# Local attention: probabilities in three transposed banks, edge rows of V by transfers, and the output product ahead of the values' projection

## The reference

```python
qkv = shift_token(x) @ wqkv
q, k = rotary_xpos(l2norm(q) * qs, l2norm(k) * ksc)
bq = q in windows of 128, * 8
bk, bv = look_around(k), look_around(v)       # the previous window and the own one: 256 keys
sim = einsum('bhwid,bhwjd->bhwij', bq, bk)
mask = (i < j) | (i > j + 128) | (j == -1)    # i, j: token numbers
out = einsum('bhwij,bhwjd->bhwid', softmax(where(mask, -max, sim)), bv)
x = x + out @ wo
```

## Time and profile before

| | us |
|---|---|
| median of 3 runs | 1901.61 (1900.96 to 1901.83) |
| the profiled execution | 1904.1 |
| its span (first to last instruction) | 1902.3 |
| PE busy | 1846.5 (97%) |
| DVE busy | 1478.6 (78%) |
| ACT busy | 1103.0 (58%) |
| POOL busy | 431.6 (23%) |

### The profile page before, as it was taken

How to read it: one execution, slowest core, us unless ns; L and a number is a source line. 1 busy time by engine, 2 the same in 40 slices (tenths; PEclk the granted TensorE clock), 3 DMA queues, 4 the chain that set the end, 5 groups by cost and what they waited for, 6 DMA issues and landing times. The chain is left out here.

```text
span 1902.3 us, 48194 instructions
## 1 busy us (share of the span) xinstructions
PE 1846.5 (97%) x17316; PEld 1605.9 (84%) x17316; DVE 1478.6 (78%) x4483; ACT 1103.0 (58%) x2551; POOL 431.6 (23%) x318
## 2 busy tenths in 40 slices
PE   8999999999999899999999999999999999989998
PEld 7879888889888788888888788877888888878887
DVE  5877867777767688888888777768888888877777
ACT  4543433433433488888988434438888888853333
POOL 0000000000000355545543000014445444501111
PEclk9999999999999999999999999999999999999999
DMA  9200000000010100000000200010000000000002
GB/s 323 72 1 2 1 1 2 1 2 1 1 70 1 52 7 4 6 6 6 4 6 11 88 12 12 11 45 5 6 6 4 6 6 6 4 23 12 12 11 94
DMA packets 47060, 44.74 MB, mean 24 GB/s; under 512 B 12479, under 2 KB 41451, under 8 KB 46958
## 3 DMA queue, kind: packets, MB, share of 16 engines
q1 hardware_dynamic: 46958, 43.33, 7.0%
HBM read 34.93 MB, written 8.39 MB: 23 GB/s over the span
## 5 line engine op out<-in xcount | busy, mean ns | idle before, releaser
L1125 ACT ACTIVATE l_probs<-l_probs,l_negmax 128x256 f32<-128x256 f32 x512 | 253.4, 498 | 83.5 <-DVE l_negmax L1235 83.5
L1083 POOL TENSOR_TENSOR l_t<-l_t,l_rnorm 128x512 f32<-128x512 f32 x128 | 131.1, 1046 | 295.2 <-DVE l_rnorm L1252 295.2
L1078 POOL TENSOR_TENSOR l_t<-l_t,l_t 128x1024 f32<-128x1024 f32 x64 | 153.2, 2394 | 126.6 <-DVE l_t L1287 126.6
L117 PE MATMUL ps<-local_w_hi,l_xT 128*128 128x512 f32 x384 | 165.2, 430 | 6.7 <-DVE l_xT L1195 3.4
L118 PE MATMUL ps<-local_w_lo,l_xT 128*128 128x512 f32 x384 | 151.9, 396 | 0.0
L119 PE MATMUL ps<-local_w_hi,l_xT 128*128 128x512 f32 x384 | 151.1, 394 | 0.0
L1413 PE MATMUL ps<-ident,l_probs 128*128 128x128 f32 x1024 | 145.5, 279 | 1.7 <-ACT l_probs L1125 1.4
L499 ACT ACTIVATE attn_exp<-ps 128x512 f32<-128x512 f32 x128 | 76.5, 600 | 116.8 <-PE ps L119 116.8
L117 PE MATMUL ps<-m_hnT_hi,ffn_w_hi 128*128 128x512 f32 (+1 forms) x352 | 141.0, 401 | 0.0
L118 PE MATMUL ps<-m_hnT_lo,ffn_w_hi 128*128 128x512 f32 (+1 forms) x352 | 138.4, 393 | 0.0
L119 PE MATMUL ps<-m_hnT_hi,ffn_w_lo 128*128 128x512 f32 (+1 forms) x352 | 138.3, 393 | 0.0
(11 more groups left out here) (252 smaller groups left out, 5790.0 us busy)
## 6 DMA issues: line engine op xcount, KB each, us to landing
tok_x<-x SPq DMA_DIRECT2D x16, 512.0 KB, 7.9
m_shifted<-shifted SPq DMA_DIRECT2D x20, 256.0 KB, 2.8
shifted<-x SPq DMA_DIRECT2D x64, 64.0 KB, 1.5
out<-x SPq DMA_DIRECT2D x8, 512.0 KB, 4.5
...
```

Of the source, the lines that this page charges most:

```text
L117: nc.tensor.matmul(out, wh, mh, start=start, stop=False, skip_group_check=True)
L1078: nc.gpsimd.tensor_tensor(t1[:], t1[:], t2[:], ALU.add).then_inc(s.summed.sem, 1)
L1083: nc.gpsimd.tensor_tensor(v, v, rn[:, a * LH:(a + 1) * LH].unsqueeze(2).to_broadcast([P, LH, DH]), ALU.mult).then_inc(s.rotated.sem, 1)
L1125: last = nc.scalar.activation(v, v, ACT.Exp, bias=nb[:, h:h + 1], scale=-1.0, accum_out=rsum[:, h:h + 1])
```

## The change

Scores and probabilities hold 192 columns for a head (`REACH`) in place of 256. A pair of heads has 384: 128 of the first head (for the low half of the queries its whole window before, for the high half the whole own window), 128 shared by the two heads' edges of 64, and 128 of the second head. So three blocks for each pair are transposed, 12 for a tile, into three banks, and ACT copies three. The scores are 32 products (128 and 64 columns) in either parity. In the values, the two halves of the queries take different weights, so there are products with 64 columns: for each half and head one with V of the whole window and one with a new tile `edge`, which holds the 64 edge rows of V for the first heads of the pairs in partitions 0 to 63 and for the second ones in 64 to 127, with zeros elsewhere (weights of 128 rows in either case). SP fills `edge` by four transfers of 64 rows x 1 KB for each tile: two from the own V when it is copied (`own_edge`), two from the window before when the values ahead are done (`next_edge`). PE waits for them (`edged`) ahead of the values. V is stored sorted by head parity. The masks are 320 wide, a window of 192 in them for each head parity; two are loaded in place of four pieces, and the even one is renewed whole by one operation. PE's output product moves ahead of V's projection.

```diff
@@ -976 @@
     HF = DH // 2
+    REACH = K.REACH
+    LOW, HIGH = slice(0, DH), slice(DH, P)
     ms = K.mlp_s[layer]
-    (xc, xt, sq, t1, t2, qt, kt, vv, pm, pt, on, spread, oth, otl), at = mem.place(
+    (xc, xt, sq, t1, t2, qt, kt, vv, edge, pm, pt, on, spread, oth, otl), at = mem.place(
         K.mlp_end, mem.end, (f"l{layer}_x", [P, 2, D], F32),
         (f"l{layer}_kT", [P, LPAIRS, 2, P], F32), (f"l{layer}_v", [P, 2, LINNER], F32),
-        (f"l{layer}_probs", [P, LPAIRS, 4 * P], F32), (f"l{layer}_probsT", [P, LPAIRS, 4 * P], F32),
+        (f"l{layer}_edge", [P, 2, LINNER], F32),
+        (f"l{layer}_probs", [P, LPAIRS, 2 * REACH], F32), (f"l{layer}_probsT", [P, 3 * LPAIRS, P], F32),
         (f"l{layer}_oT", [P, LINNER], F32), (f"l{layer}_spread", [P, LINNER], F32), (f"l{layer}_oT_hi", [P, LINNER], F32R),
...
@@ -1006 @@
     XT, RB = 5, 6
-    PT = (XT, RB, TQ, TQ + 1)
+    PT = (XT, RB, TQ)
+    THIRDS = len(PT)
...
@@ -1038 @@
+            def edge_of(which, w, tokens):
+
+                for e, rows in enumerate((LOW, HIGH)):
+                    cols = slice(e * LINNER // 2, (e + 1) * LINNER // 2)
+                    sp.dma_start(edge[rows, which, cols], vv[tokens, w, cols]).then_inc(s.edged.sem, 16)
+
+            def own_edge(t, w):
+
+                sp.wait_ge(*s.v_done.after(t + 1))
+                edge_of(0, w, LOW)
+
+            def next_edge(t, w):
+
+                sp.wait_ge(*s.o_full.after(t + 1))
+                edge_of(1, w, HIGH)
+
+            sp.wait_ge(*s.set.after(3))
+            own_edge(0, 0)
+            next_edge(0, 0)
             with sp.Fori(0, T // 2 - 2) as p:
                 for r in range(2):
+                    own_edge(2 * p + 1 + r, 1 - r)
                     store(p, r)
+                    next_edge(2 * p + 1 + r, 1 - r)
+            own_edge(T - 3, 1)
             store(T // 2 - 2, 0)
                          ).then_inc(ms.sh_in[0].sem, 16)
+            next_edge(T - 3, 1)
+            own_edge(T - 2, 0)
             store(T // 2 - 2, 1)
+            next_edge(T - 2, 0)
+            own_edge(T - 1, 1)
             store(T // 2 - 1, 0)
...
@@ -1059 @@
             nc.gpsimd.memset(vv[:, 1], 0.0).then_inc(s.set.sem, 1)
+            nc.gpsimd.memset(edge[:], 0.0).then_inc(s.set.sem, 1)
             nc.gpsimd.memset(K.w1_raw[:, :, 2 * HC * P + HR:2 * HC * P + GR], 0.0)
...
@@ -1121 @@
                     h = 2 * pair + e
-                    v = pm[:, pair, e * 2 * P:(e + 1) * 2 * P]
+                    v = pm[:, pair, e * REACH:(e + 1) * REACH]
                     last = nc.scalar.activation(v, v, ACT.Exp, bias=nb[:, h:h + 1], scale=-1.0,
-            def probs_out(t, pair):
-                wait(act, s.p_t, 4 * t + pair + 1)
-                nc.scalar.activation(pt[:, pair], ps[:, PT[pair]], ACT.Copy).then_inc(s.p_done.sem, 1)
+            def probs_out(t, k):
+                wait(act, s.p_t, THIRDS * t + k + 1)
+                nc.scalar.activation(pt[:, 4 * k:4 * k + 4].rearrange("p b q -> p (b q)"), ps[:, PT[k]],
+                                     ACT.Copy).then_inc(s.p_done.sem, 1)
...
@@ -1155 @@
                     wait(act, s.o_full, n - 2)
-                    nc.scalar.activation(vv[:, r], ps[:, V], ACT.Copy).then_inc(s.v_done.sem, 1)
+                    nc.scalar.activation(vv[:, r].rearrange("p (e m d) -> p m e d", e=2, d=DH),
+                                         ps[:, V].rearrange("p (m e d) -> p m e d", e=2, d=DH),
+                                         ACT.Copy).then_inc(s.v_done.sem, 1)
                 if c:
-                    for pair in range(LPAIRS):
-                        probs_out(n - 2, pair)
+                    for k in range(THIRDS):
+                        probs_out(n - 2, k)
                 if piece is not None:
...
@@ -1233 @@
                 last = nc.vector.tensor_tensor_reduce(
-                    pm[:, pair, e * 2 * P:(e + 1) * 2 * P], ps[:, bank, at:at + 2 * P],
-                    mask[:], -8.0, -LOWEST, ALU.add, ALU.min, nb[:, h:h + 1])
+                    pm[:, pair, e * REACH:(e + 1) * REACH], ps[:, bank, at:at + REACH],
+                    mask[:, e * P:e * P + REACH], -8.0, -LOWEST, ALU.add, ALU.min, nb[:, h:h + 1])
                 if e:
...
@@ -1260 @@
                 if b and r == 1:
-                    chain(nc.vector.tensor_scalar(mask_e[:, P:2 * P], prev[:], negs[:, bass.ds((n - 1) // 2, 1)], None,
-                                                  ALU.add))
+                    chain(nc.vector.scalar_tensor_tensor(mask_e[:], before_sel[:], negs[:, bass.ds((n - 1) // 2, 1)],
+                                                         mask_o[:], ALU.mult, ALU.add))
                 if c:
...
@@ -1387 @@
                 bank = QK if half == 0 else TQ
-                reach = (((slice(0, 3 * DH),), (slice(DH, 4 * DH),)) if own else
-                         ((slice(2 * DH, 4 * DH), slice(0, DH)), (slice(0, 2 * DH), slice(3 * DH, 4 * DH))))
+                parts = (((1 - own, slice(0, P)), (own, slice(0, P))), ((own, LOW), (1 - own, HIGH)))
+                places = ((0, DH), (P, 0))
                 for pair in (2 * half, 2 * half + 1):
-                    at = pair % 2 * 2 * P
-                    for part in range(len(reach[0])):
-                        for part_of_q in range(2):
-                            qs, keys = slice(part_of_q * DH, (part_of_q + 1) * DH), reach[part_of_q][part]
+                    for part, place in zip(parts, places):
+                        for qs, (w, keys) in zip((LOW, HIGH), part):
                             for e in range(2):
+                                at = pair % 2 * 2 * P + place[e]
                                 rows = slice(e * DH, (e + 1) * DH)
-                                last = nc.tensor.matmul(ps[qs, bank + e, at + keys.start:at + keys.stop], qt[rows, pair, qs],
-                                                        kt[rows, pair].rearrange("p w t -> p (w t)")[:, keys],
+                                last = nc.tensor.matmul(ps[qs, bank + e, at:at + keys.stop - keys.start],
+                                                        qt[rows, pair, qs], kt[rows, pair, w, keys],
                                                         start=True, stop=True)
...
@@ -1407 @@
-            def probs_t(t, pair):
-                wait(pe, s.exped, 4 * t + pair + 1)
-                for k in range(4):
-                    last = nc.tensor.transpose(ps[:, PT[pair], k * P:(k + 1) * P],
-                                               pm[:, pair, k * P:(k + 1) * P], K.ident[:])
+            def probs_t(t, k):
+                wait(pe, s.exped, 4 * t + k + 2)
+                for i in range(4):
+                    pair, block = divmod(4 * k + i, 3)
+                    last = nc.tensor.transpose(ps[:, PT[k], i * P:(i + 1) * P],
+                                               pm[:, pair, block * P:(block + 1) * P], K.ident[:])
                 last.then_inc(s.p_t.sem, 1)
-            def values():
+            def values(own):
                 for pair in range(LPAIRS):
-                    for w in range(2):
-                        for e in range(2):
-                            h = 2 * pair + e
-                            last = nc.tensor.matmul(ps[e * DH:(e + 1) * DH, OT, pair * P:(pair + 1) * P],
-                                                    vv[:, w, h * DH:(h + 1) * DH],
-                                                    pt[:, pair, (2 * e + w) * P:(2 * e + w + 1) * P],
-                                                    start=(w == 0), stop=(w == 1))
+                    for half, w in enumerate((1 - own, own)):
+                        tokens = slice(half * DH, (half + 1) * DH)
+                        for kind in range(2):
+                            for e in range(2):
+                                at = e * LINNER // 2 + pair * DH
+                                keys, block = ((vv[:, w, at:at + DH], 2 * e), (edge[:, half, at:at + DH], 1))[kind]
+                                last = nc.tensor.matmul(ps[e * DH:(e + 1) * DH, OT, pair * P + tokens.start:pair * P + tokens.stop],
+                                                        keys, pt[:, 3 * pair + block, tokens],
+                                                        start=(kind == 0), stop=(kind == 1))
                 last.then_inc(s.o_full.sem, 1)
...
@@ -1466 @@
                 if c:
-                    for pair in (2, 3):
-                        if b:
-                            wait(pe, s.qk_done, 2 * n - 3 + pair)
-                        else:
-                            wait(pe, s.masked, 4 * (n - 1))
-                        probs_t(n - 2, pair)
-                if b and not second:
-                    wait(pe, s.v_done, n - 1)
-                    project(1 - r, 2, V).then_inc(s.v_full.sem, 1)
+                    if b:
+                        wait(pe, s.qk_done, 2 * n - 1)
+                    else:
```

(22 more changed lines are left out.)

15 lines of the change are left out of this document (10 added, 5 removed).

## The result

| | before | after |
|---|---|---|
| median of 4 runs, us | 1901.28 (1900.95 to 1901.83) | 1872.5 (1871.55 to 1873.26) |
| ratio | | 0.9849 (95%: 0.9836 to 0.9863) |
| the profiled execution | 1904.1 | 1873.26 |
| its span | 1902.3 | 1871.5 |
| the two attention phases in the trace | 434.7 and 432.6 | 420.4 and 419.8 |

The kernel became 28.8 us faster. The forecast was 1879, with a low end of 1873: the direction and the account of the loop held, and the gain was underestimated; the result lies 0.5 us under the low end.

What follows compares the result with a forecast made beforehand. PE, 97% busy, was taken to bound the kernel: transposes -0.44, values +0.08, scores +0.02 make -0.34 us a tile; 64 tiles give 21.8, plus 0.9 at the start, 22.7 off 1901.6: 1879 us, range 1873 to 1892.

Steps and rivals of the forecast that it cites:

- the account of the loop: Attention loop: PE's time is a sum of instructions, -0.34 us a tile, a two-tile turn of 24.65 us.
- The swap: Output product ahead of V's projection: 0 in itself, but avoids a 0.39 us wait for ACT's V copy.
- the edges cost nothing: Edge transfers before PE's values: 2.3 to 4.0 us needed, under 4.8 available, so taken as 0.
- A values burst whose loads add to its products: Rival for PE's values: groups don't shrink with their columns, +1.75 us for +0.08, 1986 us; chance 4%.
- Transposes: PE's transposes of the probabilities, 16 become 12 a tile: -0.44 us.
- ACT's copy of qT: Ahead of PE's transposes into the bank it frees: ends 0.04 us before them, and this stays as it is.
- Values: PE's values, 16 products with 128 columns become 32 with 64: +0.08 us a tile.
- The column price: PE's values: a paired group with 64 columns costs 0.058 us, hardly over half of 0.109.
- The V copy at 897.44: PE's start of V's projection: under 0.1 us may already be lost to ACT's copy; left to the low end.
- shorter by a similar 0.3: Ends of the phases, the exponentials' step and first tile: the DVE and ACT chain shortens by about 0.3 us.
- The start of the first phase: Two mask transfers stand for four, so two issues fewer on SP: -0.9 us, once.
- POOL idle there: Added memset of the edge, about 1 us on idle POOL: delays only the MLP's weights.

Runs made afterwards that it cites:

- values_split: The kernel before with each 128-column product of the values cut into two with 64 columns, the same weights loaded for each: 1910.97 us (1.0045).
- swap_only: The kernel before with its output product moved ahead of the values' projection and nothing else: 1898.42 us against 1900.73 (0.9983).
- narrow_only: The kernel before with DVE's masked scores and ACT's exponentials over 192 of 256 columns, PE's work unchanged: 1895.93 us (0.9978).
- again: The changed kernel once more, unaltered, on the same chip as later variants: 1873.7 us (1872.8 to 1875.2).
- keep_order: The changed kernel with the values' projection left ahead of the output product: 1904.98 us (1.0021).

## Why the prediction fell short

**What held.** PE's time in the loop is a sum of its instructions, also after the change: 24.62 us for a forecast 24.65. That the two lie so close is in part luck, as the next three points show. The swap is what lets the gain through; the edges cost nothing. Between 705 and 1000 us the queues still move nothing but data, as in the earlier trace rows. A values burst whose loads add to its products would have taken 3.6 us; it took 2.02 to 2.07. The Trainium skill ("TensorE: Matmul & The Clock Gate", Part 3) says that a load overlaps with products in flight only when its row group differs; this trace disagrees.

**Transposes, sized too small.** -0.44 was forecast and -0.495 measured. I priced four transposes at 0.109 each. The group that went also waited for a copy by ACT, that of kT: in before the copy ends at 896.90 and the first transpose of the last group starts at 897.03, and this step and the next are together 0.06 us longer than 0.109 each. That ACT's copy of qT ends 0.04 us ahead of its transposes was read wrong as well: they start at 896.54, 0.13 behind the copy's end, 0.15 us a tile of waiting that neither nor the prediction shows and that is still there.

**Values, sized right in the working and too low in the sum.** The column price held: 0.058 us for a paired group with 64 columns, and the working ended at 2.00 for the burst; 2.015 was measured. Then I took +0.08, between this and the ideal, for no reason that a row gives. Ahead of the branch of the loop the burst takes 0.05 more still, which `values_split` shows growing to 0.18 in one phase: a small price for more records after all. Measured together: +0.144, which cancelled the error above; that is luck.

**The V copy at 897.44, left to the low end.** `swap_only` shows 2.3 us for the order alone. In the segments it is 0.02 to 0.03 us a tile.

**Ends of the phases, the step that failed.** The prediction took the chain through DVE and ACT to be "shorter by a similar 0.3", so that a ramp's step was worth as much as a loop's. The chain became shorter by more than that, 0.53 and 0.58 us in the first two steps of `narrow_only` and 0.53 in the last, and ACT's three copies and PE's own work gave something beside it: 2.04 us in the first three steps, where the forecast had 1.02, and 0.60 in the last, where it had 0.34. Of the 4.3 us that were missing in the two phases, the first three steps are 2.1, the last step 0.5 and what follows it 0.2. The loop, 0.03 us a tile better than forecast, is another 1.5, the start of the first phase 0.6, and the collision with the zeroing took 0.55 back.

**The start of the first phase.** I priced the masks by two issues, 0.9 us. PE's wait for DVE there fell from 3.44 to 1.02 us, as DVE doesn't wait for a mask in this profile (2.47 us in the earlier trace rows; in the other profiles with two masks up to 1.9), and the clock didn't fall behind it, another 1.2. Of these 3.6 us the zeroing took 0.5 back and longer waits for DVE and POOL further on 1.6, so the net is 1.5. With the scatter of the masks' landing, 1.5 is the figure of one execution. "POOL idle there" was true and beside the point: DVE paid.

**The range.** Its low end, 1873, stood on the values at their ideal and the V copy. By the prediction's own terms these give 1879 - 5 - 2 to 4, which is 1870 to 1872 and not 1873; and a values group at 0.060 is +5.8 us against the sum, not +3. No bound was laid on the ramps, though "a similar 0.3" was a guess. With the ramps at twice their price (-2) and the masks at the whole of the wait that stood behind them (-2.5) it would have held the result. The 0.5 us by which it was missed are less than the scatter: the same kernel gave 1873.7 in `again`, and the 27.0 us that the two phases show would have made 1901.3 - 27.0 = 1874.3. The error of 4.3 us in the phases doesn't hang on that.

## What to carry to other kernels

A cut on the engine that bounds the loop is worth its sum only if the next instruction's operand is ready that much earlier; look up when it is, and put ahead of it work whose operand is old (here 32 us hung on that, more than the whole gain). A wait of 0.1 us can stand in the loop without a bracket; hold the same group against a step in which its operand is early. Price the fill and the drain of a pipeline apart from the loop, step by step: a cut that is worth nothing in the loop can be worth half a microsecond there, and whether it adds to the others depends on the step. And a thing that is hidden is hidden by a margin: measure it in the ramps too, since three more issues were free in the loop and made PE wait for 8 us at its ends.

## What the runs showed of the chip

VectorE's rows on SBUF operands can be held by GpSimd. In the trace of after, DVE and POOL in order of time, in the loop:

```profile
887.47 1.12 DVE L1278 TENSOR_SCALAR l_ss<-l_ss 128x16 f32<-128x16 f32 x1
...
886.18 2.39 POOL L1109 TENSOR_TENSOR l_t<-l_t,l_t 128x1024 f32<-128x1024 f32 x1 [1.20 <-DVE l_t L1321]
```

The row of DVE has 16 columns and took 0.35 us on average before the change and 1.10 us after. It ends at 888.59, and POOL's at 888.57: since the add to x comes earlier now, this row falls beside POOL's addition from nearer its start and ends with it. The order alone does it: in the loop the row takes 1.13 us in `swap_only` and 0.29 in `keep_order`. That is 48 us of DVE's busy time, more than the 21 us by which its sum grew, and it costs nothing here: PE is busy all through the loop. The hold goes both ways. In after, the renewal of the mask where it starts 0.24 us ahead of POOL's multiply, then in the loop, with POOL's multiply beside it:

```profile
635.14 0.54 DVE L1297 SCALAR_TENSOR_TENSOR mask_even<-mask_sel,l_negs,mask_odd 128x320 f32<-128x320 f32 x1
...
880.81 1.02 DVE L1297 SCALAR_TENSOR_TENSOR mask_even<-mask_sel,l_negs,mask_odd 128x320 f32<-128x320 f32 x1
...
880.43 2.30 POOL L1114 TENSOR_TENSOR l_t<-l_t,l_rnorm 128x512 f32<-128x512 f32 x2 [4.12 <-DVE l_rnorm L1286]
```

POOL's two multiplies take 2.30 us there; they took 2.05 beside the shorter renewal of before. The Trainium skill says of the pair ("Trainium Architecture — The Big Picture", What this means for kernel authors) that its shared port is taken as an exclusive lock. These rows and the one beside the zeroing agree with it. Not every row of DVE is held: the add to x, which reads PSUM, takes 0.41 us beside POOL and 0.42 without it, the rotation's first product 1.22 and 1.22, the reciprocal of 8 columns 0.20 and 0.20. No run was made to separate the kinds.

A product with 64 columns and weights with all 128 rows, two column halves side by side, costs 0.0585 us with both loads; with 128 columns it is 0.109. So the loads stayed hidden down to half the columns.

A transfer of 64 KB from SBUF to SBUF, which no row of before showed, landed in 2.0 us (1.9 to 3.1) against 1.5 for one of that size from SBUF to memory, and its issue held SP's queue for 0.46 to 0.62 us.
